# A decoder block on one core: the first half of each value burst is issued two slots sooner, for ten head groups

## The reference

```
x = x + self_attention(layernorm(x))      # 16 heads of 32, causal, with biases q_b, k_b, v_b, o_b
x = x + cross_attention(layernorm(x), ctx, ctx)   # 16 heads of 32, causal, no projections, 1/sqrt(32)
x = x + relu(h @ W_up.T) @ W_down.T + (h @ W_expert) * sum(softmax(top2(h @ W_gate.T)))   # h = layernorm(x)
```

## Time and profile before

| | us |
|---|---|
| median of three runs | 713.74 (712.36 to 714.76) |
| the profiled execution | 711.97 |
| its span in the trace | 710.0 |
| TensorE busy in the span | 674.7 (95%) |
| VectorE, ScalarE, GpSimd busy | 494.6, 501.4, 256.9 |
| share of TensorE in the chain that ended last | 80% |
| steps 24 to 42 | 278.35 to 434.37 |

### The profile page before, as it was taken

How to read it: one execution, slowest core, us unless ns; L and a number is a source line. 1 busy time by engine, 2 the same in 40 slices (tenths; PEclk the granted TensorE clock), 3 DMA queues, 4 the chain that set the end, 5 groups by cost and what they waited for, 6 DMA issues and landing times.

```text
span 710.0 us, 13884 instructions
## 1 busy us (share of the span) xinstructions
PE 674.7 (95%) x4488; PEld 523.8 (74%) x4488; DVE 494.6 (70%) x1730; ACT 501.4 (71%) x1450; POOL 256.9 (36%) x391
## 2 busy tenths in 40 slices
PE   7998999999999999999889987999989999899998
PEld 6777777777787777777666755777768777677786
DVE  6568766766766776776878788767887669664632
ACT  5678877777876778787899887776588667874110
POOL 4745644333555335742564415333112102000100
PEclk9999999999999999999999999999999999999999
DMA  9763533336423573445946584633463443510101
GB/s 313 186 155 75 141 70 90 82 94 185 116 61 90 124 212 84 102 105 146 275 122 168 153 236 121 166 95 97 96 183 89 111 101 87 163 38 1 59 1 59
DMA packets 52327, 86.12 MB, mean 121 GB/s; under 512 B 8609, under 2 KB 16801, under 8 KB 52257
## 3 DMA queue, kind: packets, MB, share of 16 engines
q1 hardware_dynamic: 52256, 85.25, 46.1%
HBM read 27.55 MB, written 7.34 MB: 49 GB/s over the span
## 4 chain that ended last, share of the span: by engine, by line
PE 80%; DVE 7%; ACT 6%; issue 2%; DMA 2%; POOL 2%; SPq 1%; POOLq 0%; ACTq 0%; DVEq 0%
PE t L480 16%; PE m L519 14%; PE m L520 14%; PE m L521 14%; PE pv L513 9%; PE s L466 8%; DVE probs L682 3%; ACT probs L910 3%; ACT prob L919 1%; PE m L585 1%; DVE prob L692 1%; DMA stack<-stage 1%; POOL probs L1023 1%; PE m L480 1%; PE m L534 1%
## 5 line engine op out<-in xcount | busy, mean ns | idle before, releaser
L682 DVE CUSTOM_DVE_ANT_0 probs<-s,mask 128x128 f32<-128x128 f32 (+3 forms) x512 | 246.6, 483 | 130.7 <-PE s L466 129.0
L910 ACT ACTIVATE probs<-probs,negmax 128x128 f32<-128x128 f32 (+3 forms) x512 | 284.5, 559 | 46.1 <-DVE negmax L682 45.2
L480 PE MATMUL t<-ident,probs 128*128 128x128 f32 x1140 | 203.5, 277 | 11.4 <-ACT prob L919 6.5
L466 PE MATMUL s<-stack 96*128 96x128 f32 (+3 forms) x512 | 197.8, 394 | 5.5 <-DVE negmax L682 2.8
L1023 POOL TENSOR_SCALAR probs<-probs,rsum 128x128 f32<-128x128 f32 (+3 forms) x256 | 133.4, 539 | 176.9 <-DVE rsum L696 176.6
L919 ACT ACTIVATE prob<-t 128x384 f32<-128x384 f32 (+1 forms) x231 | 124.7, 540 | 97.7 <-PE t L480 96.7
L480 PEld LDWEIGHTS t<-ident,probs 128*128 128x128 f32 x1140 | 144.7, 141 | 60.6 <-ACT prob L919 10.5
L466 PEld LDWEIGHTS s<-stack 96*128 96x128 f32 x512 | 97.9, 191 | 18.7 <-DVE negmax L682 4.1
L910 ACT ACTIVATION_READ_ACCUMULATOR probs<-probs,negmax 128x1 f32 x512 | 98.9, 193 | 0.0
L692 DVE COPY prob<-t 128x256 f32<-128x256 f32 (+1 forms) x218 | 77.1, 354 | 30.9 <-PE t L480 29.9
L519 PE MATMUL m<-xT_hi,w_lo 128*128 128x512 f32 x192 | 78.3, 408 | 1.2 <-DVE xT_lo L750 1.2
(11 more groups left out here) (144 smaller groups left out, 946.2 us busy)
## 6 DMA issues: line engine op xcount, KB each, us to landing
stack<-stage SPq DMA_DIRECT2D x384, 128.0 KB, 2.3
xt<-in_x SPq DMA_DIRECT2D x16, 256.0 KB, 4.7
xres<-in_x SPq DMA_DIRECT2D x4, 1024.0 KB, 6.1
kraw<-in_ctxT SPq DMA_DIRECT2D x16, 256.0 KB, 3.0
cv<-in_ctx SPq DMA_DIRECT2D x16, 256.0 KB, 3.1
x<-xres SPq DMA_DIRECT2D x3, 1024.0 KB, 5.5
res<-x SPq DMA_DIRECT2D x8, 256.0 KB, 6.4
out<-res SPq DMA_DIRECT2D x2, 1024.0 KB, 4.8
```

What stands on the lines that cost most here:

```text
L466: nc.tensor.matmul(score_tile(P, i), stack[0:RS, P % 2, h, 0, chunk(qb)], stack[0:RS, P % 2, h, 1, 0:N], start=True, stop=True).then_inc(s ...
L480: mm = nc.tensor.transpose(dst[:, chunk(qb - kb)], probs[:, (2 * P + h) % 3, OFF[qb] + PART * kb:OFF[qb] + PART * kb + PART], ident[:, :])
L682: nc.vector.tensor_tensor_reduce(probs[:, (2 * P + h) % 3, OFF[qb]:OFF[qb + 1]], score_tile(P, i), mask[:, T - N:T], -SCALE, BIG, ALU.add, ...
L910: nc.scalar.activation(tile, tile, ACT.Exp, bias=negmax[:, P % 2, h, qb:qb + 1], scale=-1.0, accum_out=total).then_inc(p_exp, 1)
```

## The change

For groups 11 to 20 (`in_pieces`) value blocks 0 and 1 are issued in slots 6 and 7 of step `2G + 1`, behind the score matmul and the fill and ahead of the transposes of that slot; blocks 2 and 3 stay in slot 0 of step `2G + 2`. In the same odd steps the query transposes of a coming cross group, their high part on ScalarE and their low part on VectorE each stand one slot sooner.

```
+def in_pieces(G):
+
+    return 11 <= G <= 20
...
+                    if s % 2 == 1 and in_pieces(s // 2) and i >= PAIRS - 2:
+                        values(s // 2, i - (PAIRS - 2))
                     if s % 2 == 0 and 0 <= s // 2 - 1 < NG and i == 0:
-                        for kb in range(NT):
+                        for kb in range(2 if in_pieces(s // 2 - 1) else 0, NT):
                             values(s // 2 - 1, kb)
...
-                    if s % 2 == 1 and other((s + 3) // 2) and i == 1:
+                    if s % 2 == 1 and other((s + 3) // 2) and i == (0 if in_pieces(s // 2) else 1):
                         queries((s + 3) // 2)
...
-                    if s % 2 == 1 and other((s + 3) // 2) and i == 5:
+                    if s % 2 == 1 and other((s + 3) // 2) and i == (4 if in_pieces(s // 2) else 5):
                         query_lo((s + 3) // 2)
...
-                    if s % 2 == 1 and other((s + 3) // 2) and i == 3:
+                    if s % 2 == 1 and other((s + 3) // 2) and i == (2 if in_pieces(s // 2) else 3):
                         query_hi((s + 3) // 2)
```

## The result

| | before | after |
|---|---|---|
| median of five runs, us | 713.74 (712.36 to 715.18) | 722.94 (721.38 to 724.53) |
| ratio | | 1.0132, 95% interval 1.0112 to 1.0152 |
| the profiled execution's span, us | 710.0 | 720.7 |

The ratio is worth 9.4 us (8.0 to 10.8), where the prediction had 5.45 us. The sign was right, the size was not.

A forecast was written before the change was run, and what follows sets the result against it. TensorE bounds the kernel, busy 674.7 of 710.0 us; 2.6 + 0.7 + 0.3 + 1.05 + 0.6 + 0.2 = 5.45 us on the 713.74 us median gives 719.2 us. Forecast's own range 717 to 721.5, whole range 715.8 to 723.

The forecast's parts named there:

- The order on TensorE leaves nothing to gain behind the burst: Behind the burst, work can start sooner only by TensorE's waits between slot 6 of the odd step and the burst.
- Each further run has its price, 0.25 us: Each run of value matmuls costs TensorE 0.25 us; two more a group, 0.5 us, 5.0 us for ten groups.
- Group 16, 1.05 us: Step 33: TensorE waits 2.1 us before block 0; work left for after it 0.6 us, two runs 0.45, together 1.05.
- Group 18, 0.05 us of waiting: Group 18: block 0's copy ends just as TensorE arrives, 0.05 us on top of 0.5 us for two runs.
- Group 17: Step 35: no wait in slots 6 and 7, copy ends 0.1 us behind TensorE's arrival; 0.6 us.
- The query moves cost nothing: Query parts one slot sooner cost nothing by themselves; without the wait covering them, 0.4 us in a group at most.
- Group 20, 0.2 us: Step 41: the DMA wait can be filled, block 0 waits for the low part; blocks 2 and 3 finish 0.2 us later.
- The signs named beforehand: Step 29 slots longer, step 30 slot 0 shorter by 1.5 us; step 33 one wait; waits near 13, busy plus 5.
- the three conditions for being wrong: TensorE busy growth under 2 us, waits falling by more than 3, or step 42's end shifting unlike the whole kernel.
- the hidden change-over: Rival, chance 0.13: the price of a run is not additive, only waits are left, 0.6 us, about 714.4 us.
- The steadier feed: Rival, chance 0.06: smaller pieces let VectorE and ScalarE run ahead; if 8 us of TensorE waits went, 710.7 us.
- The clock drop: Rival, chance 0.12: behind group 16's longer wait TensorE's clock falls again for 3.4 us, losing 1.7 us: 720.9 us.

The follow-up runs named there:

- 1: The change cut to groups 11, 13, 14, 19 (1.0046), to all but groups 16 and 20 (1.0082), to group 20 alone (1.0008); ratios against the kernel before.
- 3: The whole change with value blocks 0 and 1 together in slot 7, two runs a group instead of three; 1.0026 against the kernel before.
- 2: The change for group 16 alone, timed twice (1.0044, 1.0043), and with identity transposes in its waits, two kernels (1.0027, 1.0022); ratios against the kernel before.
- experiment 5: Two edits of the kernel before: step 42's burst ahead of the score, 1.0008; some transposes of steps 41 to 43 issued twice (fastest-of-twelve profile), 1.0000.

## Why the prediction was right in sign and wrong in size

- **The order on TensorE leaves nothing to gain behind the burst.** Right. No stretch behind a burst started sooner for the move; only waits between slot 6 and the burst were filled (groups 12, 15 and 20).
- **Each further run has its price, 0.25 us.** Right in kind, 0.3 us with fills (1 and 3). In 13, without fills, it was less, 0.29 to 0.33 us for both runs where 0.55 was forecast. In 15 the score of slot 3 and others came later by 0.2 us, which was not in the sum. For groups 11 to 15 and 19 together: 3.05 us forecast, 3.16 measured. That agreement is partly luck, since single groups are off by -0.26 to +0.28 us and the errors cancel.
- **Group 16, 1.05 us.** This is the step that failed. The wait (2.02 us) and what is left for after it were as described; order and runs measured 1.4 us. But the forecast had them at full clock and kept the drop as a rival at 0.12. In all five profiles of kernels with that wait left empty the clock fell to 0.50 behind it, for all or most of the three pieces where there were three, and that cost 1.5 to 2.4 us more. The drop in the same step before was read as harmless because ScalarE bound the step. That reading was right (2), but the change took the pieces of the burst to just behind such a wait, where TensorE is what others wait for.
- **Group 18, 0.05 us of waiting.** Mis-sized: 0.68 us. For group 12 the low part was placed by the one VectorE instruction that it passes; for 18, where the output of a fill stands ahead of it, the prediction shows no such reckoning.
- **Group 17.** 1.02 us for 0.6: 0.27 us of it is a later scaling on GpSimd in slot 4 of step 35, which the query part alone shows too. "The query moves cost nothing" was wrong for it.
- **Group 20, 0.2 us.** Nearly right (1): -0.01 us at full clock.
- **The signs named beforehand.** In step 29 slots 6 and 7 grew by 1.16 and 0.95 us and slot 0 of step 30 shrank by 1.49, as forecast, and step 33 has its one long wait ahead of block 0 and none ahead of block 2. TensorE's busy time in steps 24 to 42 grew by 6.9 us for about 5, and its waits rose from 13.2 to 15.9 us, where they were to stay near 13. None of the three conditions for being wrong was met, so these signs did not catch the clock.
- **The additions.** By timing, eight groups 5.9 us, group 16 3.1, group 20 0.6: 9.6 us, against 9.4 (8.0 to 10.8) for the whole. Each term is uncertain by 1.1 to 1.4 us, so the closeness of the sum is partly luck; it shows no large part missing. Of the 4.0 us by which the forecast fell short, group 16 is 2.05 (3.1 for 1.05) and groups 17 and 18 are 0.95 (2.10 for 1.15, by the profile). The rest is no larger than these uncertainties.

Of the rivals, the hidden change-over is refuted by full steps alone (1). The steadier feed did not show: in steps 24 to 42 VectorE's waits for scores fell from 28.5 to 22.0 us, but those for transposes rose from 4.2 to 19.5, and TensorE's waits rose by 2.6 us. The clock drop is the one that happened, on top of the forecast as it said, and at 6.8 us twice as long as the earlier trace rows.

## What to carry to other kernels

Splitting a run of column-tiled matmuls cost TensorE 0.3 us for each further run here, half of that in a group without fills; move it only into a wait that is longer than that, and look for what the block itself waits for there. When an edit makes TensorE wait 2 us and puts dense work right behind, price that work at half clock as the likeliest case, not as a rival: it was so in all four profiles here with that wait. Read a delay stage by stage before reading it as one number: here the largest one sat in one group of ten, and one of the ten measured delays was not the change's at all. And before trusting a single profile, see where its execution lies among the timed ones, in time and in granted clock: the one of experiment 5 looked like a success and was the fastest of twelve.

## What the runs showed of the hardware that was not expected

- Transposes of the identity in a wait, whose result nobody reads, kept the clock up in step 33: steps 33 and 34 were at 1.00 in both kernels that had them, and with 24 added matmuls the group's delay was 2.1 us less.
- The clock in steps 41 to 43 differs from one execution to the next, also where those steps are untouched. Steps 41 and 42 of the second kernel with group 16 alone, against 1.00 in both in the kernel before:

```profile
421.09:429.55 8.46, 5.34 (x35) 3.81 (x33) 8.32 (x31) 8.42 (x28) 1.28 (x1) 0.95 1.03 285
429.55:441.07 11.52, 9.87 (x64) 5.81 (x65) 7.90 (x30) 6.25 (x20) 3.18 (x4) 0.74 0.58 138
```

  The group cost 3.43 us in that execution, 1.91 in experiment 1 and -0.01 or 0.01 in others. A single profile can be 3 us off in these two steps with no change in their code.
- What decides in which execution the drop comes there stays open. The kernel that gave TensorE 1.3 us more work a step there had no drop in its one profile, but eleven of its twelve executions had a mean clock under 1.000.
